# First attention's output product in two matmuls a tile instead of three

## The reference, cut to what matters

```
q, k, v = heads of (ln(x) Wq, [ctx Wkv ; ln(x) Wlkv])      # 4 heads of 64, 1101 keys
attn = softmax(mask(rmsnorm(q) . rmsnorm(k)))
x = x + (attn v, heads joined) Wo.T + bo
```

## Time and profile before

| | |
|---|---|
| median of three runs | 823.34 us |
| the profiled execution | 826.39 us, its span 824.5 us |
| granted TensorE clock, mean | 0.977 |
| first attention's head passes | about 39 to 343 us of the span |
| TensorE, VectorE, ScalarE busy | 92%, 64%, 48% |

### The profile page before, as it was taken

The page is one execution under the profiler, slowest core; times in us unless marked ns, Lnnn a source line. Parts: engine busy times, 40 slices in busy tenths (PEclk is TensorE's granted clock), DMA queues, the critical chain, the costliest instruction groups (busy, mean ns, idle before and its releaser), DMA issues.

```text
span 824.5 us, 12845 instructions
## 1 busy us (share of the span) xinstructions
PE 760.7 (92%) x4881; PEld 621.4 (75%) x4881; DVE 528.5 (64%) x1163; ACT 399.1 (48%) x699; POOL 319.7 (39%) x281
## 2 busy tenths in 40 slices
PE   8889989999999999999999899983799999999996
PEld 7755546656755554679889888882788999999996
DVE  7767875773677683357455498975746656667552
ACT  3655634573465344563462244433034765557551
POOL 5502001200301022066361053334235878787783
PEclk9999999999999999999999999995699999999998
DMA  7000000000000100100030201121212444544532
GB/s 186 1 0 1 1 0 1 1 0 1 1 1 2 51 4 0 52 1 3 1 98 1 103 2 52 52 77 39 103 34 78 132 119 147 129 116 110 142 33 32
DMA packets 21509, 39.31 MB, mean 48 GB/s; under 512 B 4913, under 2 KB 16905, under 8 KB 19145
## 3 DMA queue, kind: packets, MB, share of 16 engines
q1 hardware_dynamic: 14793, 30.07, 11.1%
q0 software_dynamic: 6656, 8.43, 5.9%
HBM read 29.96 MB, written 8.40 MB: 47 GB/s over the span
## 4 chain that ended last, share of the span: by engine, by line
PE 56%; DVE 15%; ACT 4%; issue 3%; POOL 3%; another core or an unknown queue 0%; DVEq 0%; ACTq 0%
PE ps L481 18%; PE ps L650 8%; PE ps L1173 5%; PE ps L1176 5%; PE ps L754 5%; PE ps L671 2%; PE ps L672 2%; PE ps L612 2%; PE ps L475 1%; DVE sm L1613 1%; DVE rep L1807 1%; PE ps L1096 1%; DVE Pb L1617 1%; DVE sm L1622 1%; POOL out_dram L2724 1%
## 5 line engine op out<-in xcount | busy, mean ns | idle before, releaser
L650 PE MATMUL ps<-PT,VA 128*65 128x512 f32 (+1 forms) x288 | 147.5, 594 | 2.8 <-ACT PT L2116 2.5
L2116 ACT ACTIVATE PT<-ps 128x512 f32<-128x512 f32 x128 | 76.0, 594 | 62.0 <-PE ps L672 61.7
L481 PE MATMUL ps<-GT,wh 128*128 128x258 f32 (+1 forms) x768 | 94.6, 284 | 0.4 <-DVE GT L1905 0.4
L481 PEld LDWEIGHTS ps<-GT,wh 128*128 128x128 f32 x768 | 92.7, 189 | 0.6 <-DVE GT L1905 0.6
L2724 POOL DMA_INDIRECT out_dram<-ye,idx x40 | 67.2, 1679 | 19.9 <-issue 10.9
L2410 ACT ACTIVATE het<-ps,b1e 128x514 f32<-128x514 f32 x64 | 44.1, 689 | 61.4 <-PE ps L481 53.7
L1940 DVE TENSOR_TENSOR he<-het,he 128x514 fp32r<-128x514 f32 x64 | 45.6, 713 | 40.2 <-ACT he L1969 38.2
L671 PE MATMUL ps<-QA,KA 128*128 128x512 f32 x144 | 67.5, 468 | 0.8 <-ACT QB L1969 0.8
L2460 POOL TENSOR_TENSOR rs<-rs,half 128x4 f32<-128x4 f32 (+2 forms) x19 | 18.2, 956 | 123.5 <-DVE rs L1214 95.6
L612 PE MATMUL ps<-KA,QA 128*128 128x368 f32 x192 | 59.2, 414 | 4.4 <-DVE x L1422 2.1
L2602 POOL DMA_INDIRECT gt<-y_dram,idx x40 | 46.3, 1158 | 43.3 <-DVE gate L1895 33.5
(11 more groups left out here) (291 smaller groups left out, 1654.2 us busy)
## 6 DMA issues: line engine op xcount, KB each, us to landing
wr<-in_w1e_dram SPq DMA_DIRECT2D x8, 1024.0 KB, 5.0
wr<-in_w2e_dram SPq DMA_DIRECT2D x8, 1024.0 KB
x<-in_x_dram SPq DMA_DIRECT2D x4, 512.0 KB, 6.2
w<-in_w_dram SPq DMA_DIRECT2D x2, 1024.0 KB, 4.7
y_dram<-yr SPq DMA_DIRECT2D x3, 512.0 KB, 3.0
out_dram<-x SPq DMA_DIRECT2D x3, 512.0 KB, 4.1
b2r<-in_b2r_dram SPq DMA_DIRECT2D x8, 128.0 KB, 3.3
gt<-y_dram,idx POOLq DMA_INDIRECT x40
```

What stands on the lines that cost most here:

```text
L481: op = pe.matmul(o, l, r, start=n == 0, stop=n == len(calls) - 1)
L650: pe.matmul(bank[6 + hf][0:65, :], VA[b][0:K, kt, h, :], PT[u % 4][0:K, :], start=kt == 0, stop=kt == 8).then_inc(p_pv, 1)
L2116: a.activation(PT[u % 4][0:K, :], bank[4 + u % 2][0:K, :], ACT.Exp, bias=0.0 if K == 128 else mcol[:, b:b + 1]).then_inc(a_exp, 1)
```

## The change

`wo` and `OT` grow from 65 to 128 partitions. OT[0] now holds the high half in rows 0 to 63 and the low half beneath it in rows 64 to 127; wo[0] holds the high weights twice. One matmul of 128 rows thus makes high x high and low x high. OT[1] holds the high half again in rows 0 to 63, the denominator in rows 64 and 65 and the denominator's remainder in row 96, against low weights, low bias row and two copies of the high bias row in wo[1]; one matmul of 97 rows makes high x low and all that belongs to bias and denominator. The values get a second column of ones. ScalarE copies twice a half, VectorE subtracts twice a half. GpSimd clears two blocks of 64 partitions, and SyncE copies rows of wo inside SBUF with three DMAs, with two waits.

```diff
-        wo = [RA(f"wo{i}", [65, H0, 258], F32R)[:, :, :] for i in range(2)]
+        wo = [RA(f"wo{i}", [128, H0, 258], F32R)[:, :, :] for i in range(2)]
-        VA = [RA(f"VA{i}", [128, 9, H0, 65]) for i in range(2)]
+        VA = [RA(f"VA{i}", [128, 9, H0, 66]) for i in range(2)]
-        OT = [RA(f"OT{j}", [65, S], F32R) for j in range(2)]
+        OT = [RA(f"OT{j}", [128, S], F32R) for j in range(2)]
...
-                    pe.wait_ge(a_whi, 3)
                     pe.wait_ge(g_wlo, 3)
-                three(bank[m][:, 0:258], [((OT[0][:, c], OT[1][:, c]), (wo[0][:, h, :], wo[1][:, h, :]))]).then_inc(p_wo, 1)
+                    pe.wait_ge(d_rows, 112)
+                pe.matmul(bank[m][:, 0:258], OT[1][0:97, c], wo[1][0:97, h, :], start=True, stop=False)
+                pe.matmul(bank[m][:, 0:258], OT[0][:, c], wo[0][:, h, :], start=False, stop=True).then_inc(p_wo, 1)
...
-                    pe.matmul(bank[6 + hf][0:65, :], VA[b][0:K, kt, h, :], PT[u % 4][0:K, :], start=kt == 0,
+                    pe.matmul(bank[6 + hf][0:66, :], VA[b][0:K, kt, h, :], PT[u % 4][0:K, :], start=kt == 0,
...
-                    v.tensor_tensor(OT[1][:, qc], bank[6 + hf][0:65, :], f(OT[0][:, qc]), ALU.subtract).then_inc(v_ot, 1)
+                    v.tensor_tensor(OT[0][64:128, qc], bank[6 + hf][0:64, :], f(OT[0][0:64, qc]), ALU.subtract)
+                    v.tensor_tensor(OT[1][96:97, qc], bank[6 + hf][64:65, :], f(OT[1][64:65, qc]), ALU.subtract).then_inc(v_ot, 1)
...
-                        a.wait_ge(g_wlo, 3)
-                    copy(OT[0][:, qc], bank[6 + hf][0:65, :]).then_inc(a_ot, 1)
+                        a.wait_ge(g_init, 7)
+                    copy(OT[0][0:64, qc], bank[6 + hf][0:64, :])
+                    copy(OT[1][0:66, qc], bank[6 + hf][0:66, :]).then_inc(a_ot, 1)
...
-                g_.memset(va[:, :, :, 64:65], 1.0).then_inc(g_init, 1)
+                g_.memset(va[:, :, :, 64:66], 1.0).then_inc(g_init, 1)
...
             low(wv[1], wv_in, wv[0], 2)
+            g_.wait_ge(g_wlo, 2)
+            step(g_.memset(f(wo[1][64:128, :, :]), 0.0))
+            settle()
             step(g_.memset(wo_in[:, :, 256:258], 0.0))
...
-            low(wo[1], wo_in, wo[0], 3)
+            low(wo[1][0:65, :, :], wo_in, wo[0][0:65, :, :], 3)
...
             low(wqk[1][:, :, 256:512], wqk_in[1], wqk[0][:, :, 256:512], 4)
+            g_.wait_ge(g_wlo, 4)
+            g_.memset(f(OT[1][64:128, :]), 0.0).then_inc(g_init, 1)
+            g_.wait_ge(g_init, 7)
...
             load_x(3)
+            sp.wait_ge(g_wlo, 3)
+            for p in (65, 96):
+                sp.dma_start(f(wo[1][p:p + 1, :, :]), f(wo[0][64:65, :, :])).then_inc(d_rows, 16)
+            sp.wait_ge(d_rows, 96)
+            sp.dma_start(f(wo[0][64:128, :, :]), f(wo[0][0:64, :, :])).then_inc(d_rows, 16)
```

More of the change, by code:

```diff
@@ L2333, in scalar_program @@
             a.wait_ge(g_wo, 1)
-            halved(wo[0], wo_in, (d_rows, 64))
+            halved(wo[0][0:65, :, :], wo_in, (d_rows, 64))
             values(0, 2, 6)
```

## The result

The changed kernel takes 839.68 us (median of 4 runs, 836.85 to 840.75) against 823.16 us of the kernel before (4 runs, 822.95 to 825.36): a ratio of 1.0189, interval 1.0159 to 1.022. It is slower by 16.5 us, where +9.8 was forecast, and inside the range of 823 to 841. Its profiled execution took 839.93 us (span 837.7).

What follows compares the result with a forecast made beforehand. TensorE was taken to set the pace in the head passes. Places +10.4 and +3.55, start-up +0.15, gain -4.3 make +9.8 on 823.34, so 833.1 us; own range 828 to 838, stated range 823 to 841.

Steps and rivals of the forecast that it cites:

- The gain: Output tiles on TensorE: one matmul less saves 0.12 us in each of 36 of 64 tiles, 4.3 us.
- The second copy: ScalarE at each half: a second copy of OT delays VectorE's start by 0.50 us.
- The row: VectorE at each half: the second subtraction, one row by 512, costs 0.69 us by its length.
- the rival of small additions: At each half: one-row subtraction near 0.2 us, second copy 0.3, so +0.8 in all, 824.1 us; chance 0.15.
- The places: Sixteen moves of a half out of PSUM: eight at full price 10.4 us, seven partial 3.55, head 7's end nothing.
- a full place: A place without slack behind OT, where the whole lengthening, mostly 1.35 us, lands on TensorE; eight were counted.
- The start-up: Before the head passes: GpSimd's longer clearing beside VectorE's cast costs between 0 and 0.95 us, taken as 0.15.
- the full price of heads 1 and 2: Middles of heads 1 and 2: the added chain lands wholly on TensorE, 1.35 us and 1.23 us.
- rivals C and D: C: third product hidden, nothing gained, 837.4 us, chance 0.13. D: all sixteen places full price, no gain, 845.9 us, chance 0.07.

Runs made afterwards that it cites:

- e3: The kernel before without the product of OT's low half with wo's high half, and no additions: 819.97 us against 823.69, ratio 0.9958.
- e7: The changed kernel plus idle transposes on TensorE in the long waits of heads 1 and 2: 833.57 us, against 837.54 without them on the same chip.
- e2: The changed kernel with ScalarE's first copy into OT[1] and the copy into OT[0] made behind the next exponential, nothing left out: 828.08 us, ratio 1.0048.
- e6: The changed kernel without the one-row subtraction and with the copy into OT[0] made behind the next exponential: 820.44 us, ratio 0.997.
- e5: As e2, with the one-row subtraction moved behind the next tile's x except in head 2's middle, nothing left out: 834.49 us, ratio 1.0125.
- e8: As e2 but for head 7's later copy, with the one-row subtraction put at once or behind a tile by place, nothing left out: 824.33 us, ratio 1.0011.
- e4: The kernel before with its three products, plus a second ScalarE copy and a one-row VectorE subtraction at each half: 840.65 us, ratio 1.0196.
- e9: As e8, plus idle transposes on TensorE in the middles of heads 1 and 2, nothing left out: 826.13 us, ratio 1.0033.

## Why the prediction came out as it did

- **The gain.** 4.3 us was taken for 36 of 64 tiles at 0.12; e3 measured 3.7, with a fall of the clock in its profile. Where no wait lies between, a tile takes 360.14 - 359.90 = 0.24 us, for the 0.36 of the earlier trace rows (timeline of TensorE in the changed kernel, head 7):

```profile
359.90 0.28 PE L634 MATMUL ps<-wo,OT 97*128 97x258 f32 x1
360.02 0.28 PE L635 MATMUL ps<-wo,OT 128*128 128x258 f32 x1
360.14 1.54 PE L481 MATMUL ps<-xt,w1e 128*128 128x512 f32 x6
```

- **The second copy.** 0.50 was taken, 0.48 measured. The Trainium skill, "ScalarE: Activation LUTs", section "What ACT_TABLE_LOAD costs", with its overlap of neighbours came to an estimate of 0.52: here the trace agrees to 0.04 us, and the pair of QA copies (0.60 each) was the wrong neighbour to go by. Only one of that pair shifts its rows (line 2046 of the kernel before), so the shift is not shown to be the reason.
- **The row.** 0.69 was taken by its length, 0.69 measured; the rival of small additions (824.1) falls with it. The first subtraction into shifted rows lets its successor start after 0.70 (0.73 taken).
- **The places.** With the clock whole (e7), the middles measured 1.28, 1.06, 1.01, 0.16, 1.01, 1.19, 1.07 and 0.31 us, for 1.35, 1.35, 1.23, 0.15, 1.1, 1.35, 1.35 and 0.45 in the working; the starts of heads 1 to 7 0.56, 1.41, 0.48, 0.10, 0.45, 1.19 and 1.29, for 0.75, 1.35, 0.5, 0.3, 0.5, 1.35 and 0.9. The measured shifts hold the tiles of their stretch, 0.12 less each. Fourteen of the fifteen were right to 0.3 us; the start of head 7 is rather a full place. As a whole e7 stands 10.2 us above the kernel before (833.57 - 823.35), where the sum said 9.8. This agreement of e7 with the forecast is the check on its mechanism.
- **The start-up.** 0.15 was taken, -0.6 measured in the first profile and +0.5 in that of e7, whose start-up is the same: the size of this term is not settled. In the changed kernel the instruction of VectorE that grew beside GpSimd's subtraction is the cast (1.52 us), and the subtraction that TensorE waits for took its plain 0.69 us though the clearing lay beside all of it (timeline; against the 2.17 us of the earlier trace rows). The Trainium skill, "SBUF — State Buffer", section "SBUF: two separate sides", has a port that GpSimd and some VectorE forms take by turns, and counts a VectorE operation with two inputs in SBUF only against a GpSimd operation that reads SBUF. A clearing reads nothing there, and the trace agrees: the 0.69 us stand beside the clearing, the 2.17 us of before beside a GpSimd subtraction.

```profile
15.96 1.36 POOL L2483 TENSOR_TENSOR wv<-PT,wv 128x512 fp32r<-128x512 f32 x1
16.08 1.52 DVE L1237 CAST xt<-PT 128x512 fp32r<-128x512 f32 x1
...
17.38 1.12 POOL L2630 MEMSET wo<- 64x1032 f32 x1
17.63 0.69 DVE L1239 TENSOR_TENSOR xt<-PT,xt 128x512 fp32r<-128x512 f32 x1
...
18.38 1.70 PE L481 MATMUL ps<-wqk,xt 128*128 128x256 f32 x12 [0.33 <-DVE xt L1239]
```

- **What was missing.** The sum priced each wait at its own length, at one clock. The term that it lacked is the clock behind the waits of heads 1 and 2: 4.0 us in the paired runs (3.3 of it in these two middles by their profiles), and in the first profile, with falls twice as long, about 2.5 more by the two middles (4.03 + 3.84 against 2.69 + 2.68). With 4.0 it comes to 9.8 + 4.0 + 2.5 = 16.3 of the 16.5, with 3.3 to 15.6. The last of these terms rests on one profile and was not tested by itself. The step that failed is thus the full price of heads 1 and 2: I followed each new wait up to TensorE's start and not beyond, and so put what follows it at nothing. That the one in head 1 would stand 0.8 us of work ahead of the wait of 1.8 us for yb could be read in the timeline of before.

That the range held the time was luck: 839.68 lies outside the forecast's own 828 to 838, and the range reached 841 for rivals C and D, neither of which happened.

## What to carry to other kernels

Price an addition at its length and not its rows: a one-row remainder costs an engine as much as the tile that it completes, and here that instruction cost 7.3 us (e2 against e6) where the products had gained 3.7 (e3). When an instruction is moved behind another, ask which buffers it still holds; e5 moved a wait onto the bank's next user. And where a new wait is put near an old one on TensorE, price it twice, at the clock before and at the lower clock for the stretch behind it.

## What was not expected of the hardware

- TensorE's granted clock fell to half for 3.4 or 6.8 us in or behind waits, most of them of 1.7 to 2.8 us, in the middles of heads 1 and 2, and each fall there cost 1.6 us (3.4 long) or 2.8 to 3 us (6.8 long) against the same place without a fall. The wait's length alone did not decide it: in e5 a fall of 6.8 us stands behind waits of 0.45 and 0.81 us, the wait of 1.7 us in head 2 had a fall behind it in e8 and none in e2, and 1.8 us in head 1 of the kernel before had none.
- A short fall at 39 to 43 us at the start of the head passes is in the profiles of e2, e4, e6 and the changed kernel run again, and not in those of the others or of before; with it the exponentials from the fourth on are 0.8 to 1.0 us late, without it 0.5 to 0.7 us early (0.5 late in e7). So one profile against one profile carries an error of this size.
- Idle transposes in the waits gave 4.0 us in e7; in e9 they took the one fall away in the profile, and yet its median was 1.8 us above that of e8.
